# A sixteen-batch attention and expert kernel: scan in blocks of 64 tokens, compact scores, denominators by a 32-column sum and a DMA round trip, and a new order of the work

## The reference, cut to what matters

```python
x = layernorm(h); hh = layernorm(x, ln1)
# xq, xk, xv, xg: hh mixed with its shift by one token
q = exp(rmsnorm(xq @ Wq.T));  k = exp(rmsnorm(xk @ Wk.T))
v = xv @ Wv.T;                g = sigmoid(xg @ Wg.T)
lam = exp(-exp(time_decay))             # one factor per channel
A = lam * A + k_t (outer) v_t           # per head, 32 x 32, for each token
z = lam * z + k_t
S_t = q_t . A;  Z_t = q_t . z
att = g * (S / Z) @ Wo.T
```

## Time and profile before

| | |
|---|---|
| median of 3 runs | 1093.0 us (1091.03 to 1094.89) |
| span of the profiled execution | 1090.0 us |
| instructions | 44778 |
| TensorE busy | 1058.7 us, 97% |
| VectorE busy | 886.6 us, 81% |
| ScalarE busy | 702.5 us, 64% |
| GpSimd busy | 293.5 us, 27% |
| mean granted TensorE clock | 0.990 |

### The profile page before, as it was taken

How to read it: one execution, slowest core, us unless ns; L and a number is a source line. 1 busy time by engine, 2 the same in 40 slices (tenths; PEclk the granted TensorE clock), 3 DMA queues, 4 the chain that set the end, 5 groups by cost and what they waited for, 6 DMA issues and landing times.

```text
span 1090.0 us, 44778 instructions
## 1 busy us (share of the span) xinstructions
PE 1058.7 (97%) x18851; PEld 800.2 (73%) x18851; DVE 886.6 (81%) x2749; ACT 702.5 (64%) x1258; POOL 293.5 (27%) x177
## 2 busy tenths in 40 slices
PE   6789999999999999999999999999999999999987
PEld 6668677877767778687877867777786777868664
DVE  6889788888988879788887988878788887979642
ACT  3357676576666757576575767657676675758643
POOL 5322132331223222132332223232122322213120
PEclk9799999999999999999999999999999999999999
DMA  5532133122312322132232312313242232214110
GB/s 179 168 91 88 52 94 102 60 89 72 125 51 74 106 76 89 51 127 70 65 97 73 108 51 78 117 59 89 60 130 57 74 105 77 71 51 127 52 39 18
DMA packets 51510, 91.55 MB, mean 84 GB/s; under 512 B 9552, under 2 KB 26608, under 8 KB 51312
## 3 DMA queue, kind: packets, MB, share of 16 engines
q1 hardware_dynamic: 51312, 88.69, 26.7%
HBM read 19.50 MB, written 9.78 MB: 27 GB/s over the span
## 4 chain that ended last, share of the span: by engine, by line
PE 95%; DVE 2%; ACT 1%; issue 1%; POOL 0%; DMA 0%; SPq 0%; DVEq 0%; ACTq 0%; POOLq 0%
PE bank L999 13%; PE bank L1004 11%; PE bank L1148 11%; PE bank L1170 10%; PE bank L1141 10%; PE bank L1176 10%; PE bank L1103 7%; PE bank L1078 4%; PE bank L1081 3%; PE bank L1121 3%; PE bank L1164 3%; PE bank L1086 3%; PE bank L1125 3%; PE bank L1041 3%; PE bank L1030 2%; PE bank L1056 1%
## 5 line engine op out<-in xcount | busy, mean ns | idle before, releaser
L1170 PE MATMUL bank<-xa,f1w 128*128 128x512 f32 (+1 forms) x256 | 120.5, 575 | 0.9 <-issue 0.9
L1148 PE MATMUL bank<-w,hid 128*128 128x128 f32 x1024 | 119.7, 275 | 1.5 <-ACT hid L565 1.5
L1141 PE MATMUL bank<-c,w 128*128 128x512 f32 (+1 forms) x256 | 119.2, 570 | 0.9 <-ACT c L559 0.9
L1148 PEld LDWEIGHTS bank<-w,hid 128*128 128x128 f32 x1024 | 116.9, 192 | 2.9 <-ACT hid L565 2.9
L539 ACT ACTIVATE px<-bank 128x512 f32<-128x512 f32 (+1 forms) x128 | 72.8, 568 | 63.5 <-PE bank L1086 55.2
L419 POOL TENSOR_TENSOR rr<-vv,nhalf 128x4 f32<-128x4 f32 x32 | 32.4, 1012 | 294.9 <-DVE vv L823 294.9
L565 ACT ACTIVATE hid<-bank 128x512 f32<-128x512 f32 (+1 forms) x128 | 70.2, 565 | 63.7 <-PE bank L1141 61.9
L1176 PE MATMUL bank<-hid,f2w 128*128 128x512 f32 (+1 forms) x256 | 107.5, 563 | 0.0
L1103 PE MATMUL bank<-qx,ki 128*32 128x16 f32 x7680 | 102.2, 193 | 1.5 <-DVE ki L866 1.5
L1103 PEld LDWEIGHTS bank<-qx,ki 128*32 128x32 f32 x7680 | 92.7, 110 | 13.7 <-issue 13.7
L804 DVE COPY_PREDICATED px<-mask,bank 128x512 f32<-128x512 uint32 (+1 forms) x128 | 88.5, 691 | 13.5 <-ACT px L539 13.5
(11 more groups left out here) (142 smaller groups left out, 2447.9 us busy)
## 6 DMA issues: line engine op xcount, KB each, us to landing
qx<-qq SPq DMA_DIRECT2D x256, 96.0 KB, 2.2
hs<-hs SPq DMA_DIRECT2D x32, 532.0 KB, 3.9
v<-v_f SPq DMA_DIRECT2D x16, 512.0 KB, 6.0
gz<-gate_f SPq DMA_DIRECT2D x16, 512.0 KB, 3.0
xT<-in_xT SPq DMA_DIRECT2D x16, 468.5 KB, 3.2
f1w<-in_fc1T SPq DMA_DIRECT2D x16, 256.0 KB, 3.2
f2w<-g_dram SPq DMA_DIRECT2D x16, 256.0 KB, 3.3
out<-t_sum SPq DMA_DIRECT2D x16, 256.0 KB, 2.5
```

The lines of the kernel that those rows point to most:

```text
L1141: mm(dst[:, 0:width[g]], w1[:, P * j:P * j + P], c1[:, cols(g)], start=True, stop=True).then_inc(w1_ok, 1)
L1148: last = mm(dst[:, P * i:P * i + P], hid[:, j, P * m:P * m + P], w2[:, j, :], start=(j == 0), stop=(j == 3))
L1170: mm(dst[:, 0:width[g]], f1w[:, P * j:P * j + P], xa[:, cols(g)], start=True, stop=True).then_inc(f1_ok, 1)
```

## The change

- Blocks of BLK = 64 tokens carry the state, not tiles of 128. There are 15 blocks and NST = 14 states (7 before). `us` makes 14 of them, `chain` and `states` handle 14. `scan` runs each of its two products once per block, with 64 columns. `v` becomes two buffers, `v[0]` with the first 64 tokens of each tile and zeros, `v[1]` with the others, filled by two DMAs in `hand_v`; `us` reads them.
- Scores are needed only within 64 tokens. The 256-column products, their levels in `qx` (3 x 256 columns become 2.5 x 256) and `kw` go. The scores of a tile are compact, [128, 4 heads, 64], and BETWEEN and DIAG lie in one bank. Two banks are used in turn. `pairs_a` and `pairs_b` become `pairs`, and `pxs` waits for the whole of it. Within `pairs` the order of windows is new.
- `zts` uses `hsel`, a 32-column weight, with q times z as the moving operand, and gives 128 rows (tile and head) of 128 tokens. `denominators` takes 128x128. `spread_rz` and `rTs` go. `rz_out` writes the result to DRAM and `rz_back` reads it back in four DMAs, each row to 32 partitions, into the memory of `zq`. `zscan` of the next batch therefore waits for `gate`.
- All engines' lists, the queue of SyncE and the sharing of banks 0 to 4 are ordered anew. TensorE's stages are counted 1 to 3 and not 0 to 2, which is a name only.

The core of the diff:

```diff
+BLK = P // 2
+PAIRS, SOUT = (5, 6), 7
...
+    blocks = [-(-windows[c] // 2) for c in range(TILES)]
+    NBLK = sum(blocks)
+    NST = NBLK - 1
...
-                sp.dma_start(v[:, :, :], v_f[:, :, :]).then_inc(v_in, 16)
+                for o in (0, 1):
+                    rows = slice(BLK * o, BLK * o + BLK)
+                    sp.dma_start(v[o][rows, :, :], v_f[rows, :, :]).then_inc(v_in, 16)
...
+            def rz_out(b):
+                before(sp, rb_in, b, 64, 64)
+                sp.wait_ge(rz_ok, nth(b, 1, 1))
+                sp.dma_start(rz_dram[:, :, :].rearrange("m x n -> (m x) n"), rz[:, :]).then_inc(rzd_in, 16)
+
+            def rz_back(b):
+                sp.wait_ge(rzd_in, nth(b, 16, 16))
+                for hd in range(HEADS):
+                    row = rz_dram[:, HEADS * hd, :].rearrange("m (o n) -> o m n", o=1)
+                    sp.dma_start(rb[HD * hd:HD * hd + HD, :, :], row.to_broadcast([HD, TILES, P])).then_inc(rb_in, 16)
...
             def gate(b, g):
-                dve.wait_ge(rT_ok, nth(b, 2, g + 1))
+                dve.wait_ge(rb_in, nth(b, 64, 64))
...
             def zts(b):
                 dst = free_bank(pe, b, "zt")
                 pe.wait_ge(qz_ok, nth(b, 1, 1))
-                for m in range(TILES):
-                    last = mm(dst[:, HEADS * m:HEADS * m + HEADS], zq[:, P * m:P * m + P], heads1[:, 0:P:HD], start=True, stop=True)
+                for i in (0, 1):
+                    for w in range(TILES // 2):
+                        m = 2 * w + i
+                        last = mm(dst[WIN * w:WIN * w + WIN, 0:P], hsel[:, i, :], zq[:, P * m:P * m + P], start=(i == 0), stop=(i == 1))
                 last.then_inc(zt_ok, 1)
...
-                pe.wait_ge(v_ok, nth(b, 2, 2))
-                for c in range(NST):
+                pe.wait_ge(v_in, nth(b, 32, 32))
+                for i in range(NST):
                     for hd in range(HEADS):
                         r = slice(HD * hd, HD * hd + HD)
-                        last = mm(dst[r, c:HD * NST:NST], kcT[:, c, r], v_f[:, c, r], start=True, stop=True)
+                        last = mm(dst[r, i:HD * NST:NST], kcT[:, i // 2, r], v[i % 2][:, i // 2, r], start=True, stop=True)
...
+                if c >= 2:
+                    pe.wait_ge(px_ok, nth(b, TILES, c - 1))
...
+                even, odd = range(0, windows[c], 2), range(1, windows[c], 2)
+                for w in even:
+                    over_half(w)
                 for j in range(1, NE):
...
+                    for w in odd:
+                        over_eight(w, j)
+                for j in range(EIGHT + NE - 1):
+                    for w in even:
+                        last = over_eight(w, j + 1) if j < NE - 1 else in_eight(w, j - NE + 1)
+                    if j < EIGHT:
+                        for w in odd:
+                            in_eight(w, j)
+                last.then_inc(pr_ok, 1)
...
+                opened = False
+                for o in range(blocks[c]):
+                    i, t = 2 * c + o, s0 + BLK * o
+                    if i:
+                        for hd in range(HEADS):
+                            r = slice(HD * hd, HD * hd + HD)
+                            mm(S[r, t:t + BLK], ab[:, i - 1, r], qc[:, BLK * i:BLK * i + BLK], start=not opened, stop=False, skip_group_check=True)
+                        opened = True
+                pe.wait_ge(px_ok, nth(b, TILES, c + 1))
+                for o in range(blocks[c]):
+                    t = s0 + BLK * o
                     for hd in range(HEADS):
                         r = slice(HD * hd, HD * hd + HD)
-                        mm(S[r, s0:s0 + n], ab[:, c - 1, r], qc[:, P * c:P * c + n], start=True, stop=False, skip_group_check=True)
```

TensorE's new order of the scan's steps in a round, with the work of the other batches between them: pairs 0; us; pairs 1; pairs 2, zts, scan 0, pairs 3, scan 1; pairs 4, scan 2, scan 3, pairs 5; pairs 6, pairs 7, scan 4, scan 5; scan 6, scan 7. VectorE's new order around it:

```diff
+                if (b := at(2)) is not None:
+                    merge(b, 1)
+                if (b := at(1)) is not None:
+                    stats1(b, 1)
+                if (b := at(2)) is not None:
+                    denominators(b)
+                if (b := at(3)) is not None:
+                    x_attn(b, 0)
+                if (b := at(1)) is not None:
+                    variance1(b)
+                if (b := at(3)) is not None:
+                    normed3(b, 1)
+                if (b := at(2)) is not None:
+                    merge(b, 2); inside(b, 1)
                 if (b := at(1)) is not None:
                     normed(b)
                 if (b := at(2)) is not None:
-                    merge(b, 3)
+                    between(b, 1); gate(b, 0); gate(b, 1); merge(b, 3)
```

SyncE's new list:

```diff
             def body(at):
+                if (b := at(2)) is not None:
+                    hand_h1(b)
+                if (b := at(3)) is not None:
+                    expert(b)
+                if (b := at(2)) is not None:
+                    spread(b, 1); hand_h2(b)
                 if (b := at(0)) is not None:
                     samples(b)
                 if (b := at(2)) is not None:
...
+                    rz_out(b); spread(b, 2); rz_back(b); hand_gate(b); spread(b, 3)
+                if (b := at(3)) is not None:
+                    store(b, 0)
+                if (b := at(1)) is not None:
+                    spread(b, 0); hand_v(b)
+                if (b := at(3)) is not None:
+                    store(b, 1)
```

More of the change, by code:

```diff
@@ L207, in program @@
         place = {name: (i, n) for i, users in enumerate(USES) for n, (name, _) in enumerate(users)}
-        spare = [bank[i] for i in range(8) if i not in [BETWEEN, DIAG] + [place[n][0] for n in ("dct0", "dct1", "nT0", "nT1")]]
+        spare = [bank[i] for i in range(8) if i not in [*PAIRS] + [place[n][0] for n in ("dct0", "dct1", "nT0", "nT1")]]
         EARLY = 5
@@ L499, in vcopy @@
                 act.wait_ge(vm_ok, nth(b, 2, g + 1))
[L500 removed]
+                before(act, v_in, b, 32, 32)
                 before(act, u_ok, b, 1, 1)
@@ L1185, in body @@
+                if (b := at(3)) is not None:
+                    n2Ts(b, 1)
+                if (b := at(2)) is not None:
+                    gates(b, 0); gates(b, 1)
                 if (b := at(1)) is not None:
-                    qkv(b, "k", 1)
+                    dcts(b, 0)
+                if (b := at(3)) is not None:
+                    w1s(b, 1, 0); w1s(b, 1, 1)
                 if (b := at(2)) is not None:
-                    n2Ts(b, 0); scan(b, 5); pairs_a(b, 7); pairs_b(b, 7); w1s(b, 0, 0); scan(b, 6); scan(b, 7)
@@ L1244, in body @@
                 if (b := at(2)) is not None:
-                    f1s(b, 1, 1)
+                    pairs(b, 4); scan(b, 2); scan(b, 3); pairs(b, 5)
+                if (b := at(3)) is not None:
+                    oTs(b, 0); f1s(b, 1, 0); f1s(b, 1, 1); f1s(b, 1, 2)
                 if (b := at(1)) is not None:
-                    scan(b, 3); pairs_a(b, 4); pairs_b(b, 4)
+                    qkv(b, "k", 0); qkv(b, "k", 1)
+                if (b := at(3)) is not None:
+                    f1s(b, 1, 3)
@@ L1248, in body @@
+                if (b := at(1)) is not None:
+                    qkv(b, "q", 0)
                 if (b := at(2)) is not None:
-                    f1s(b, 1, 2); f1s(b, 1, 3); oTs(b, 0)
+                    attends(b, 0)
                 if (b := at(1)) is not None:
-                    attends(b, 0); pairs_a(b, 5); pairs_b(b, 5); scan(b, 4)
+                    qkv(b, "q", 1)
                 if (b := at(2)) is not None:
+                    pairs(b, 6); pairs(b, 7); scan(b, 4); scan(b, 5)
+                if (b := at(3)) is not None:
```

466 lines of the change are left out of this document (198 added, 268 removed), and 10 rows, old and new, of the table USES.

## The result

The changed kernel takes 1152.6 us (median, 1149.6 to 1159.4) where the kernel before takes 1093.4 us on the same chip (1091.0 to 1094.9). The ratio is 1.0548, with a 95% interval of 1.0509 to 1.0588. It is slower by 5.5%, where a gain of 7% was forecast, and lies 95 us above the upper end of the predicted range of 994 to 1058 us. The profiled execution has a span of 1148.7 us.

The account below looks back on a forecast made before the run. TensorE, busy 97%, was taken as the bound until VectorE became the limit. Terms cut a round from 64.65 to 58.6 us, 59.6 with coupling; over 16 rounds, plus 3 at the ends, 1012, as median 1015 us; range 994 to 1058.

Parts of the forecast that it names:

- A: Theory formed after the measurement, not forecast: TensorE runs out of instructions in dense runs of small matmuls.
- B: Theory formed after the measurement, not forecast: VectorE is held up behind GpSimd's states, 2.6 us a round.
- The pairs of a tile: Products of a tile on TensorE: 1.03 us instead of 1.56, seven tiles saving 3.7 us a round.
- two-group pace: Rival: a tile's products take 1.38 us, not 1.03, giving 1038 us; chance 0.15.
- Scans: TensorE's scan tiles: two 64-column blocks cost no more than one tile; +0.1 us a round, bounds -0.1 and +0.8.
- Stretches: TensorE's runs of 32-column-weight matmuls: three fewer at 0.28 us each, -0.85 us a round.
- GpSimd's states: Between us and scan 0: states double from 2.54 to about 5 us, covered by TensorE's 8.8 us of other work.
- VectorE's slack and coupling: VectorE busy 52.1 us of a 58.6 us round; fitting the new order costs +1.0 us, bounds 0 and +3.4.
- The round trip: Denominators through DRAM to gate: 7.6 us, covered by 10.5; no cost, bounds 0 and 0.9. Slower-kernel rival: 0.04.
- v in halves: us waits for two DMAs of v: 5.1 to 8.1 us against 7.2 of cover; priced 0, bound 0.9 a round.
- The rival of late halves: Rival: us waits 0.9 us for v_in in each round, giving 1029 us; chance 0.10.
- Ends: One-time start of the kernel: larger table dec and an added copy cost +3 us, bounds 0 and 6.

Follow-up runs that it names:

- e10: e5 with TensorE's list put back to the dense one of the changed kernel; 1168.3 us, ratio 1.0696.
- e4: Kernel before with four runs of 512 matmuls (32-column weight; 16, 32, 64, 128 moving columns) added at its end; 27.0 us for 16 columns, 28.16 for 128.
- e9: e5 with the states written by GpSimd again; 1145.7 us, ratio 1.0490.
- e5: Changed kernel with TensorE's dense runs spread apart, states written by ScalarE and the first tile's norm earlier on VectorE; 1096.6 us, ratio 1.0040.
- e8: Kernel before with GpSimd's states lengthened and VectorE's qlev of the second half moved beside them; 1171.2 us, ratio 1.0725.
- e6: e5 with VectorE's gates moved behind merge 3 and x_attn 1; 1094.4 us, ratio 1.0011.
- e1: Changed kernel with only TensorE's list reordered, its dense runs cut apart by 128-column work; 1150.1 us, ratio 1.0513.
- e12: e6 with two of four state copies behind ScalarE's c, and x_attn ahead of the denominators on VectorE; 1095.7 us, ratio 1.0031.
- e13: e12 with ScalarE's hcopy put ahead of the last two copies of the states; 1111.5 us, ratio 1.0184.
- e7: Changed kernel without the products of windows 2 and 3 of each tile, so output is incomplete; 1080.1 us, ratio 0.9887.

## Why the prediction was wrong

The step that failed is the one in which busy time became time: "in the steady part each microsecond of TensorE work taken out of a round is gained, until VectorE ... becomes the limit". A third limit stood between them, the rate at which TensorE gets instructions, and the change raised their number, from 1178 to 1310 matmul records a round with as many weight loads, while packing them into fewer, denser stretches. I priced the second half of us at +0.48 us for 112 instructions, 4.3 ns each, and the tile at 1.03 for 184, from rows of short, isolated runs, and did not ask how many such runs stand in a row. 6.1 of the 6.9 us of idle time in a round carry the mark of A. e10 shows it without B, e4 by itself.

Beside it a second step failed: GpSimd's longer `states` was taken as covered, and what it does to VectorE was put at nothing. With a spread list this costs 49 us (e9 against e5).

By terms, per round, each part measured in the 800 us from the start of one matmul to the start of the next, idle time left out, before and after:

| part | predicted | before | after | change |
|---|---|---|---|---|
| products of the tiles | -3.7 | 11.95 | 9.00 | -2.95 |
| scans | +0.1 | 3.56 | 4.26 | +0.70 |
| us | +0.5 | 0.54 | 1.31 | +0.77 |
| zts | -1.2 | 1.80 | 0.53 | -1.27 |
| transposes (rTs) | -0.9 | 7.66 | 6.42 | -1.24 |
| all else (fewer stretches) | -0.85 | 39.14 | 40.10 | +0.96 |
| work of a round | -6.05 | 64.65 | 61.6 | -3.0 |
| idle (coupling) | +1.0 | 0.1 | 6.9 | +6.8 |

- *The pairs of a tile*: right in kind. A tile in mid-stretch, from its first kw matmul to the scan's, is 1.1 us; the two-group pace (1.38) is refuted. The rows, from the chain of the changed kernel:

```profile
548.53 0.16 PE bank L1097
548.69 0.09 PE bank L1102 x6
...
548.97 0.14 PE bank L1102 x5
549.14 0.47 PE bank L1107 x46
549.66 0.23 PE bank L1139 x14
549.89 0.22 PE bank L1146 x16
550.12 0.21 PE bank L1139 x10
550.32 1.29 issue
```

 The same lines end in the stall: a tile, a scan and the start of the next, and then 1.29 us of nothing.
- *Scans* and *us* were mis-sized by 0.6 and 0.3 us. In the rows above a scan tile takes 0.23 + 0.22 = 0.45 us, as reckoned, but over all eight it is 4.26 / 8 = 0.53 where it was 3.56 / 8 = 0.45: the upper bound of +0.8 was the right end. *zts* and *rTs* came as reckoned or better.
- *Stretches*: the 0.85 us did not show. All other matmuls grew by 0.96 us. The clock explains that: TensorE was busy for 41.6 us in the 800 at the lower level, which adds at most 20.8 us to the work, 1.8 a round. With the means of the matmuls outside those stretches in place of all, the work of a round is 59.9 us and all else 38.7, against 39.1 before. So the stretches saved about 0.4 us and not 0.85, and the clock took it back. The scans are 4.1 us by the same means.
- *GpSimd's states, "covered, with 2 us to spare"*: the cover on TensorE's side held, scan 0 rarely waited. But the instruction was priced only by who waits for its result, not by what it does to VectorE while it runs. That is B, 2.6 us a round in VectorE's queue, worth 49 us once A is gone (e9 against e5).
- *VectorE's slack and coupling*: its busy time came to 661.9 / 11.67 = 56.7 us a round where I had 52.1; the blocked `qlev` is 2.6 of the difference and the blocked `nrm` and `nb` 1.9. e8 shows how false the argument "no wait in 800 us today" was: a lack of waits says that the lists fit, not that there is room.
- *The round trip*: 7.6 us were booked, 10.7 measured (the reciprocal at 537.35, the gate at 549.02, less 0.94), near the upper bound of 11.4. The price, 1.9 us of VectorE's idle time a round, was above the bound of 0.9, but where e6 takes it away it was worth about 2 us in all. The gate waited in all 16 rounds, which the prediction had named as the proof of this rival; the sign was too weak, since the wait could go (e1, e6) with next to no gain.
- *v in halves*: us waited for v once in the whole run, 1.3 us at 46.7 us, and never in the 800. The rival of late halves did not come true. Whether the halves landed sooner than one copy would have is not shown, so the rule that pointed to this rival is not tested by it.
- *Ends*: the sum of rounds accounts for the result: 16 x (68.5 - 59.6) = 142 us against 1148.7 - 1012 = 137.

None of the rivals with a slower end had this mechanism, so the 4% for "slower" had only the round trip in it. That e5, without both causes, still takes 1097 and not 1015 is the rest of the error: its work is 61.9 us a round (with the spread list's own stretches), and 2.5 us idle, 64.4 in all. Waits of 1.5 us move from engine to engine when one is taken away (e12, e13), and VectorE is still held up by about 1.6 us a round beside GpSimd's `t_sum`. Whether an order exists with dense enough work and no starved runs isn't settled by these runs.

## What to carry to other kernels

When a change cuts work into more and smaller instructions, count instructions beside microseconds in each run of them, and compare with the fastest run that the present trace shows to last. For an instruction made longer on GpSimd, ask which VectorE operations will run beside it, not only who waits for its result. When two suspects each give nothing on removal, remove both before acquitting either: here neither alone gave anything and both, with one norm moved, gave 56 us.

## What the runs showed of the hardware that I had not expected

- TensorE gets 256 instructions per 3.47 us, in some blocks 3.75 (e4), so that matmuls with a 32-column weight and up to 64 columns, four side by side, cannot be kept up: 512 of 16 columns take 27.0 us (1103.67 to 1130.71) and of 128 columns 28.16 us.
- VectorE's product of two SBUF buffers, 0.7 us long, took up to 3.78 us beside one GpSimd instruction, and three of them 5.00 instead of 1.36 (e8). Small ones suffer as well, 0.17 us becoming 1.13. Not delayed beside the same instruction were the sum that reads PSUM (0.67 us beside, 0.68 elsewhere) and the statistics of one buffer (0.27 and 0.28).
- Idle gaps can cost twice: the granted clock was 1.2 GHz for 44 us of the 800 in the changed kernel and for 44 us in e9, each time during or just behind a gap of 1.8 to 3.5 us, and at no time in e6, whose gaps are below 1 us but for three. It does not follow every gap: the changed kernel has 37 over 1.3 us and 12 such stretches, e13 twelve of about 2.1 us and two, e12 fifteen of 1.3 us or more and none.
- Half of a tile's products (e7), on two of four column groups, took 8.0 of the 9.0 us that all take.
